# Top-2 experts that add into one row of each node by accumulating indexed writes, instead of writing two rows that the norms add

## The reference, cut

```python
m = segment_sum(h[src], dst) * rsqrt(deg_in)          # aggregate over the edges
x = m @ W_gc + b_gc + feats @ W_res + b_res           # called x1 in the kernel
vals, idx = top_k(x @ Wg + bg, 2); gates = softmax(vals)
...                                                   # each expert: gelu(rows @ w1 + b1) @ w2 + b2
core = zeros((N, D)).at[tok].add(gate * y_of_expert)  # two experts add to every node
y = x + core
mean = y.mean(0); var = ((y - mean) ** 2).mean(0)
ref = (y - mean) * rsqrt(var + 1e-5) * gamma + beta
out = layernorm(feats + ref)
```

## Time and profile before

| | |
|---|---|
| time, median of 3 runs | 3281.04 us (3276.84 to 3282.05) |
| the profiled execution | 3277.43 us |
| its span, first to last instruction | 3275.6 us |
| DVE, PE, POOL busy | 2021.3, 2694.6, 2045.8 us |
| DMA, mean over the span | 160 GB/s |

### The profile page before, as it was taken

The page is one execution under the profiler, slowest core; times in us unless marked ns, Lnnn a source line. Parts: engine busy times, 40 slices in busy tenths (PEclk is TensorE's granted clock), DMA queues, the critical chain, the costliest instruction groups (busy, mean ns, idle before and its releaser), DMA issues. The chain is left out here.

```text
span 3275.6 us, 60296 instructions
## 1 busy us (share of the span) xinstructions
PE 2694.6 (82%) x14773; PEld 2014.2 (61%) x14906; DVE 2021.3 (62%) x7071; ACT 1198.1 (37%) x2854; POOL 2045.8 (62%) x2077
## 2 busy tenths in 40 slices
PE   0664888888898888988889889869999999999750
PEld 0552655555565555555555555558888888888640
DVE  6997556556556555565566556555555555555698
ACT  0895122222222222222222222234444444444339
POOL 4686677777777777777777777725555555555300
PEclk9886999999999999999999999989999999999885
DMA  2847545545545455455454554544444544444477
GB/s 72 256 150 244 177 138 161 172 141 162 163 146 160 140 162 171 139 163 168 142 163 137 173 164 126 163 130 141 143 136 148 175 133 135 146 147 137 143 295 247
DMA packets 314409, 524.66 MB, mean 160 GB/s; under 512 B 45928, under 2 KB 229994, under 8 KB 312589
## 3 DMA queue, kind: packets, MB, share of 16 engines
q0 software_dynamic: 97968, 261.94, 27.1%
q1 hardware_dynamic: 216026, 259.90, 23.8%
q10 hardware_dynamic: 259, 0.91, 0.1%
HBM read 405.08 MB, written 121.76 MB: 161 GB/s over the span
## 5 line engine op out<-in xcount | busy, mean ns | idle before, releaser
L1589 POOL DMA_INDIRECT work<-h_table,src_cols x1431 | 1360.2, 951 | 461.5 <-issue 421.9
L1981 PE MATMUL ps<-work 128*128 128x257 f32 x3126 | 991.9, 400 | 184.1 <-DMA work<-h_table,src_cols 161.7
L1981 PEld LDWEIGHTS ps<-work 128*128 128x128 f32 x3126 | 545.5, 192 | 503.6 <-issue 362.7
L2127 POOL DMA_INDIRECT picked<-ys,places x228 | 248.2, 1088 | 363.0 <-DVE ys L2197 343.3
L2252 PEld LDWEIGHTS ps<-xst,work 128*128 128x128 f32 x3648 | 443.8, 193 | 27.8 <-issue 16.0
L2252 PE MATMUL ps<-xst,work 128*128 128x128 f32 x3648 | 447.6, 276 | 10.8 <-issue 10.1
L2259 PE MATMUL ps<-work,hid 128*128 128x256 f32 x1824 | 436.9, 383 | 0.6
L1852 PE MATMUL ps<-none_w,none 128*128 128x512 bf16 x1142 | 436.7, 382 | 0.0
L2108 ACT ACTIVATE hid<-ps,b_cols 128x128 f32<-128x128 f32 x912 | 316.1, 367 | 172.4 <-PE ps L2252 127.1
L2259 PEld LDWEIGHTS ps<-work,hid 128*128 128x128 f32 x1824 | 329.7, 191 | 46.0 <-ACT hid L2108 11.1
L1655 DVE TENSOR_TENSOR logits<-ps,gate_bias 128x64 f32<-128x64 f32 x98 | 22.0, 225 | 511.4 <-ACT acc L1536 511.4
(11 more groups left out here) (347 smaller groups left out, 4067.4 us busy)
## 6 DMA issues: line engine op xcount, KB each, us to landing
work<-in_L_gnn_w_dram SPq DMA_DIRECT2D x128, 512.0 KB, 4.5
picked<-work SPq DMA_DIRECT2D x14, 1792.0 KB, 8.2
pk<-picked SPq DMA_DIRECT2D x13, 1792.0 KB, 12.9
work<-h_table,src_cols POOLq DMA_INDIRECT x1431, 2.8
x_ahead<-work SPq DMA_DIRECT2D x105, 128.0 KB
work<-x_ahead SPq DMA_DIRECT2D x105, 128.0 KB, 2.7
acc<-h_table SPq DMA_DIRECT2D x14, 896.0 KB, 6.1
x_beta<-xr_x SPq DMA_DIRECT2D x98, 128.0 KB, 1.9
```

Source lines behind the costliest of these rows:

```text
L1589: pool.indirect_dma_start(out=got[:, c % RING, 0:D], out_offset=None, in_=h_table[0:NT * P, :], in_offset=bass.IndirectOffsetOnAxis(ap=src ...
L1981: mm = nc.tensor.matmul(ps_flat[:, bank(t, k, w[0])], hot[:, (2 * t + (k >= HALF)) % HOTS, k % HALF if k >= HALF else k, :], got[:, c % RI ...
L2127: pool.indirect_dma_start(out=picked[:, :], out_offset=bass.IndirectOffsetOnAxis(ap=places[:, u:u + 1], axis=0), in_=ys[:, u, :], in_offse ...
```

## The change

`picked` and its 14 stores of zeros are gone. A DRAM table `y_rows` has one row for each node and 128 spare rows. It begins as x1: at each store of `x1_rows`, SP issues a second store of the same tiles to `y_rows` (20 more DMAs, 98 tiles of 128 KB). The scatter of a turn becomes an accumulating one: the DMA adds `ys` to the rows that stand in the table. The two experts of a node add to the same row, so a scatter now waits for the landing of the scatter before it. A slot without a node gets a spare row of its own lane, and all 128 rows are written.

In `norms`, a load brings a group of `y_rows` (896 KB) straight into `acc3`, over x1; the two additions are gone, and the mean is subtracted after the load, group by group. The subtraction of 3 groups at the end of `experts` is gone too. Loads wait for no buffer, only for the landing of the one that used the same semaphore four loads before. The steps of `table` that made the old places are one fewer.

```diff
+                    sp.dma_start(by_lane(y_rows[0:NT * P, :])[:, a:b, :], acc3[:, a:b, 0:D]).then_inc(rows_out, 16)
...
-                    if slot % SET == 2 and slot < NT:
-                        clear_picked(slot // SET)
...
-                nc.vector.scalar_tensor_tensor(place_of, row_of, float(TOP_K), second_of, ALU.mult, ALU.add).then_inc(table_set, 1)
+                nc.vector.scalar_tensor_tensor(place_of, first_of, unused[:, 0:1], row_of, ALU.mult, ALU.add).then_inc(table_set, 1)
                 dve.wait_ge(table_set, 9)
-                nc.vector.tensor_tensor(place_of, place_of, first_of, ALU.add).then_inc(table_set, 1)
-                dve.wait_ge(table_set, 10)
...
-                def send(n, u):
+                def send(n, j, u):
                     pool.wait_ge(y_set, n + 2)
                     pool.sem_inc(carrier, 1)
-
-                    pool.indirect_dma_start(out=picked[:, :], out_offset=bass.IndirectOffsetOnAxis(ap=places[:, u:u + 1], axis=0),
-                                            in_=ys[:, u, :], in_offset=None, bounds_check=PLACES - 1,
-                                            oob_is_err=False).then_inc(y_sent[u % 2], 16)
+                    if not isinstance(n, int) or n > 0:
+                        pool.wait_ge(y_sent[(u - 1) % 2], 32 * j + (u + 1) // 2 * 16)
+                    pool.sem_inc(carrier, 1)
+                    pool.indirect_dma_start(out=y_rows[:, :], out_offset=bass.IndirectOffsetOnAxis(ap=places[:, u:u + 1], axis=0),
+                                            in_=ys[:, u, :], in_offset=None, compute_op=ALU.add).then_inc(y_sent[u % 2], 16)
...
-                for g in range(CENTRED):
-                    rows = acc3[:, g * GT:(g + 1) * GT, 0:D]
-                    nc.vector.tensor_tensor(rows, rows, y_total[:, :].unsqueeze(1).broadcast_to([P, GT, D]), ALU.subtract)
...
-                    if g >= B:
-                        sp.wait_ge(second_added, adds(g - B))
-                    sp.dma_start(pk[:, g % B, :, :], rows_of(rows, g)).then_inc(pk_in[g % B], 16)
+                    if g > B:
+                        sp.wait_ge(y_in[g % B], 16 * ((g - 1) // B))
+                    sp.dma_start(group(g), rows_of(y_rows, g)).then_inc(y_in[g % B], 16)
...
                     if g > 0:
-                        dve.wait_ge(pk_in[g % B], 16 * (g // B + (g % B > 0)))
+                        dve.wait_ge(y_in[g % B], 16 * ((g - 1) // B + 1))
                     for n, (a, b) in enumerate(FIRST_PARTS if g == 0 else parts(g)):
                         if g == 0:
                             dve.wait_ge(first_in[n], 16)
-                        done += 1
-                        add(g, a, b, done)
-                    if g + UPFRONT < NG:
-                        centre(g + UPFRONT)
+                        nc.vector.tensor_tensor(group(g, a, b), group(g, a, b), mean[:, :].unsqueeze(1).broadcast_to([P, b - a, D]),
+                                                ALU.subtract).then_inc(centred, 1)
```

More of the change, by code:

```diff
@@ L101, in gnn_layer @@
     x_beta = nc.dram_tensor("x_beta", [NPAD, D], F32).ap()
-    picked = nc.dram_tensor("picked", [NPAD * TOP_K, D], F32).ap()
+    y_rows = nc.dram_tensor("y_rows", [NPAD + P, D], F32).ap()
     x_ahead = nc.dram_tensor("x_ahead", [(AHEAD + EXTRA) * P, D], F32).ap()
@@ L407, in gnn_layer @@
             with nc.cleanup_on_exit():
-                aggregate(nc, x, W_res, b_gc, b_res, W_gc, Wg, bg, b1, beta, h_table, x1_rows, x_beta, picked, degree0, flag_i, zeros_out, y_total, acc3, work, ident, ones,
+                aggregate(nc, x, W_res, b_gc, b_res, W_gc, Wg, bg, b1, beta, h_table, x1_rows, x_beta, y_rows, degree0, flag_i, y_total, acc3, work, ident, ones,
                           iota_f, place_lo, src_cols, rel_cols, where, valid, f_edge, f_lanes, x_ahead, extra_f_in, early_set, table, base_of, b1_cols, load_weights, ps,
                           N=N, D=D, X=X, H=H, KD=KD, KH=KH, AW=AW, CH=OCH, PER=PER, EARLY=EARLY, LATE=LATE, NT=NT, LAST=LAST)
-            experts(nc, x1_rows, picked, w1s, w2s, b2s, w_in, load_weights, ident, ones, table, base_of, b1_cols, y_total, acc3, ps, N=N, D=D, X=X, H=H, KD=KD, KH=KH,
-                    ROW=ROW, PLACES=NPAD * TOP_K)
+            experts(nc, x1_rows, y_rows, w1s, w2s, b2s, w_in, load_weights, ident, ones, table, base_of, b1_cols, y_total, acc3, ps, N=N, D=D, X=X, H=H, KD=KD, KH=KH,
+                    ROW=ROW)
         kept.close()
-        norms(nc, x_beta, picked, gamma, out, y_total, acc3, ones, valid, ps, N=N, D=D, NT=NT, LAST=LAST)
+        norms(nc, x_beta, y_rows[0:NPAD, :], gamma, out, y_total, acc3, ones, valid, ps, N=N, D=D, NT=NT, LAST=LAST)
 def group_edges(nc, src, dst, edge_src, edge_dst, rows_s, rows_d, iota_f, ones, ps, E, CH, CL, RJ, NT):
@@ L1259, in _, with aggregate @@
                                          stop=True).then_inc(summed, 1)
-def aggregate(nc, x, W_res, b_gc, b_res, W_gc, Wg, bg, b1, beta, h_table, x1_rows, x_beta, picked, degree0, flag_i, zeros_out, y_total, acc3, work, ident, ones, iota_f,
+def aggregate(nc, x, W_res, b_gc, b_res, W_gc, Wg, bg, b1, beta, h_table, x1_rows, x_beta, y_rows, degree0, flag_i, y_total, acc3, work, ident, ones, iota_f,
               place_lo, src_cols, rel_cols, where, valid, f_edge, f_lanes, x_ahead, extra_f_in, early_set, table, base_of, b1_cols, load_weights, ps,
@@ L1333, in aggregate @@
         lane = t2("lane", [P, 1], F32)
+        unused = t2("unused", [P, 1], F32)
+        NO_ROW = (BIG - TOP_K * P) >> 8
+        assert TOP_K * P == 256 and ((BIG - TOP_K * P) >> 1) % P == 0 and NO_ROW < NT * P
         off_graph = t2("off_graph", [P, NT], F32)
@@ L2011, in _, with experts @@
                 list_places(NT - 1)
-def experts(nc, x1_rows, picked, w1s, w2s, b2s, w_in, load_weights, ident, ones, table, base_of, b1_cols, y_total, acc3, ps, N, D, X, H, KD, KH, ROW, PLACES):
+def experts(nc, x1_rows, y_rows, w1s, w2s, b2s, w_in, load_weights, ident, ones, table, base_of, b1_cols, y_total, acc3, ps, N, D, X, H, KD, KH, ROW):
     with ExitStack() as part:
@@ L2266, in _, with norms @@
                 nc.tensor.matmul(ps[:, 5, 0:D], ones[:, :], y_total[:, :], start=True, stop=True).then_inc(mean_done, 1)
-def norms(nc, x_beta, picked, gamma, out, mean, acc3, ones, valid, ps, N, D, NT, LAST):
+def norms(nc, x_beta, y_rows, gamma, out, mean, acc3, ones, valid, ps, N, D, NT, LAST):
     with ExitStack() as part:
@@ L2345, in _ @@
             def _(sp):
-                rows = picked.rearrange("(n k) d -> n (k d)", k=TOP_K)
                 for g in range(NG):
@@ L2375, in _ @@
                 for q in range(B):
-                    sp.wait_ge(second_added, adds(NG - B + q))
                     load_x(q)
@@ L2392, in _ @@
                 nc.vector.tensor_copy(last_ones[:, :], valid[:, NT - 1:NT].broadcast_to([P, P])).then_inc(last_ones_set, 1)
-                def centre(g):
-                    nc.vector.tensor_tensor(group(g), group(g), mean[:, :].unsqueeze(1).broadcast_to([P, GT, D]),
-                                            ALU.subtract).then_inc(centred, 1)
-                def add(g, a, b, n):
-                    nc.vector.tensor_tensor(group(g, a, b), group(g, a, b), pk[:, g % B, a:b, 0:D], ALU.add).then_inc(first_added, 1)
-                    dve.wait_ge(first_added, n)
-                    nc.vector.tensor_tensor(group(g, a, b), group(g, a, b), pk[:, g % B, a:b, D:2 * D], ALU.add).then_inc(second_added, 1)
-                for g in range(CENTRED, UPFRONT):
-                    centre(g)
-                done = 0
                 for g in range(NG):
-                    if g >= CENTRED:
-                        dve.wait_ge(centred, g - CENTRED + 1)
                     if g > 0:
-                        dve.wait_ge(pk_in[g % B], 16 * (g // B + (g % B > 0)))
+                        dve.wait_ge(y_in[g % B], 16 * ((g - 1) // B + 1))
                     for n, (a, b) in enumerate(FIRST_PARTS if g == 0 else parts(g)):
@@ L2425, in _ @@
                 dve.wait_ge(scale_set, 1)
-                dve.wait_ge(second_added, adds(NG - 1))
+                dve.wait_ge(centred, adds(NG - 1))
                 def times_scale(g):
```

38 lines of the change are left out of this document (16 added, 22 removed).

## The result

The changed kernel takes 3541.07 us (median of 5 runs, 3532.5 to 3546.57) against 3281.04 us: ratio 1.079, 95% interval 1.078 to 1.081. It is slower, by 260 us, where 180 us were forecast. The profiled execution has a span of 3544.8 us, 269.2 us more than before.

What follows compares the result with a forecast made beforehand. POOL's issue was taken to bound aggregate, PE the experts, DVE the norms' first pass. Chained scatters +211, end of experts -4.4 and first pass -29.7 make +177 us on 3281: 3458, rounded 3460 us, range 3290 to 3690 us.

Steps and rivals of the forecast that it cites:

- The new wait: Experts, POOL: each scatter waits for the previous landing, making a chain with links of 4.89 us against 3.96, +211 us.
- A plain chain has almost no slack: Experts: chained plain scatters would take 3.79 us for each turn, where 3.96 us are there.
- Disturbance by weight loads: Experts: weight loads in flight a third of the time add 1.8 us then, 0.6 us on the mean link.
- What accumulating adds: Experts: extra time e for the scatter to read its target before writing, taken as 1.1 us.
- quiet link: Experts: start of one scatter to the next without weight loads: plain 2.3 + 0.89 us, plus 1.1 us for accumulating.
- its bounds: Experts: accumulating's extra time lies between 0.5 us and 1.85 us, read from gathers; chance 0.68.
- e = 0.3 us: Experts: accumulating's extra time by the skill's fit, target's 128 KB counted once more; whole change then at 3277 us.
- The end of the experts: Last scatter to the norms' first load: 3.7 us instead of 8.1, so -4.4 us.
- The first pass: Norms: PE becomes the longest, 53 us instead of 82.7, so -29.7 us.
- The hidden chain: Rival, experts: target reads overlap, e between 0 and 0.35 us, fully hidden 3247 us; chance of faster 0.09.
- e = 2.8 us: Rival, experts: accumulating costs a whole second transfer, link 6.59 us, 3844 us; within the 0.12 chance above 1.85 us.
- PE's granted clock: Rival, experts: a less busy PE loses clock, 4.9 us a turn at 0.76, 7.5 at 1.2 GHz; within the 0.12 chance.

Runs made afterwards that it cites:

- e2: The kernel before, with its scatters accumulating onto the zeros of picked and no further wait: 3378.6 us, ratio 1.0288 to 1.0316.
- e1: The kernel before, plus only each scatter's wait for the landing of the one ahead, still overwriting: 3305.4 us, ratio 1.0067 to 1.0095.
- e6: The changed kernel with expert weights loaded during the stage cut to slivers of 16 columns: 3406.0 us, ratio 1.0378 to 1.0405.
- e3: The kernel before with accumulating scatters and the wait for the one ahead, old norms: 3565.9 us, ratio 1.0859 to 1.0889.
- e8: The changed kernel without the wait for the scatter ahead and with weights cut to slivers: 3215.3 us, ratio 0.9786 to 0.9813.

## Why the prediction was right, and where a term was off

**The new wait.** Right. The scatter waits for a DMA 221 times of 228, ACT's copies wait longer, PE is at 82%. One reading behind it was not exact: that GpSimd never waits for a landing in the kernel before. Its scatters stood behind late gathers 5 times, 9.9 us of 800, and this small wait is the one that grows in e2.

**A plain chain has almost no slack.** Right in substance: the estimate of 3.79 us against PE's 3.96 us left 0.17 us, and e1 measured 4.09 us, so there was none. Single late landings, up to 5.4 us, are probably not all smoothed by the two turns of `ys` in the ring; that was not tried by itself.

**Disturbance by weight loads, 0.6 us for each link.** Right on the mean: 0.61 us between the changed kernel and e6. Its two factors were both off, and that they cancel is luck: the forecast put 1.8 us on a third of the links, the trace has 2.35 us on 64 of 227, 28%, which is 0.66 us by the two groups of links above.

**What accumulating adds, e = 1.1 us.** This is the term that was mis-sized. The quiet link was forecast as 2.3 + 1.1 + 0.89 = 4.29 us and is 4.67 us in e6, where the landing is 3.8 us and the rest, 0.87 us, is the dispatch as forecast. So e is 3.8 - 2.3 = 1.5 us, inside its bounds, and 227 x 0.38 = 86 us are the miss of 81. The scatter's own issue on GpSimd grew by 0.57 us (1577 - 1008 ns), which the prediction named as a sign but did not price; how much of the 1.5 us it makes was not separated. The choice "just under the middle", because a gather's tail contains a completion that the scatter has already, was wrong in effect: the value stands three quarters of the way up, (1.5 - 0.5) / (1.85 - 0.5).

The Trainium skill, "DMA: Bandwidth & Descriptors", section "Anatomy of one DMA", has a fit for a DMA from GpSimd by its bytes; the estimate from it, with the target's bytes counted once more, was e = 0.3 us. The measurement decides against that estimate: 1.5 us.

**The rest of the sum.** The end of the experts is -3.0 us (forecast -4.4): the first load follows the last scatter by 5.07 us, a little over the 5 us named, mostly because from the last landing, seen at 3390.1 us, to that load it is 1.3 us and not 0.26. The first pass is 53.7 us (forecast 53), with 44.81 / 196 = 0.229 us for a matmul (forecast 0.226), `aggregate` 0. All right but for that 1.4 us.

**Rivals.** The hidden chain is out; e = 2.8 us is out. PE's granted clock was 0.94 on the mean of the stage, between its levels of 1.2 and 2.4 GHz and near the upper, with PE idle for 18% of the time; but GpSimd waits for its DMA and not for PE's results, so nothing in the profile puts that on the path, and in e6, at a granted clock of 1.00, the links are still 4.67 us.

**What the prediction did not see** lies beside its sum: even unchained, accumulating costs 0.48 us a turn here (e2), through gathers that land late beside the weights' burst. The two costs don't add: the wait alone is worth 0.13 us, accumulating alone 0.48, both 1.27 (e3).

## What to carry to other kernels

When a change makes transfers wait for each other, write the link of the new chain as landing plus dispatch, and compare it with the pace of the bounding engine; here 4.67 us against 3.83 us decided, whatever the stage behind it gained. An operation that is harmless alone can cost much beside another: price it with the largest burst beside it on the DMA engines, and look at who waits for its neighbours' landings, not only for its own. A burst of prefetches with much lead can be issued in pieces that wait for each other; that gave 0.7% here on an otherwise unchanged kernel, and took too long where the pieces landed late.

## What the hardware showed that was not expected

- An accumulating scatter of 128 rows of 1 KB occupies GpSimd for 1577 to 1714 ns instead of 977 to 1172 ns (medians of the runs), and lands 3.8 to 3.9 us after its start instead of 2.3 to 2.6 us.
- For each turn of a gather and a scatter, GpSimd's queue in e2 carries 191 packets instead of 96 and takes 1.46 us of all 16 DMA engines instead of 0.78 us, with no more counted bytes (0.242 against 0.245 MB).
- Accumulating scatters on disjoint rows that don't wait for the one ahead don't slow a turn by themselves (e8: 3.83 us apart). Since a quiet one lands after 3.8 us, this run says little about two of them in flight for long.
- Beside a chain of accumulating scatters, one set of weights of 1152 KB makes about one link late, 6.97 us instead of 4.62 us.
